# Attention and channel-mixing block: the first products directly behind score 3, the weight differences in other banks, and the first two projections later

## The reference

```python
def layernorm(x): return (x - mean(x)) / sqrt(var(x) + 1e-5)

def attention(x, weight):                 # b=4, t=1024, c=128, nh=16, hs=8
    y = x.reshape(b, t, nh, hs).transpose(0, 2, 1, 3)
    attn = softmax(einsum('bhtk,bhsk->bhts', y, y) / sqrt(hs))
    o = einsum('bhts,bsc->bhtc', attn, x)            # all 128 channels for each head
    return o.transpose(0, 2, 1, 3).reshape(b, t, nh * c) @ weight

def channel_mix(x, W_r, W_k, W_v, mu_r, mu_k):
    x_prev = x shifted by one token, zeros ahead of it
    xr, xk = mu_r*x + (1-mu_r)*x_prev, mu_k*x + (1-mu_k)*x_prev
    return sigmoid(xr @ W_r.T) * (relu(xk @ W_k.T)**2 @ W_v.T)

x = x + layernorm(attention(layernorm(x), weight))
x = x + layernorm(channel_mix(layernorm(x), ...))
```

## Time and profile before

| | |
|---|---|
| time, median of 3 | 944.18 us (943.57 to 948.45) |
| profiled execution | 950.29 us, of it a span of 948.5 us |
| TensorE busy | 914.9 us (96%) |
| VectorE busy | 850.3 us (90%) |
| ScalarE busy | 753.4 us (79%) |
| GpSimd busy | 320.2 us (34%) |

### The profile page before, as it was taken

The page is one execution under the profiler, slowest core; times in us unless marked ns, Lnnn a source line. Parts: engine busy times, 40 slices in busy tenths (PEclk is TensorE's granted clock), DMA queues, the critical chain, the costliest instruction groups (busy, mean ns, idle before and its releaser), DMA issues.

```text
span 948.5 us, 17874 instructions
## 1 busy us (share of the span) xinstructions
PE 914.9 (96%) x6065; PEld 441.9 (47%) x6065; DVE 850.3 (90%) x1117; ACT 753.4 (79%) x1048; POOL 320.2 (34%) x485
## 2 busy tenths in 40 slices
PE   3999999999999999999999999999999999999995
PEld 2444444444544444444444444544544444444453
DVE  7889898899898899989988979989889899898887
ACT  6787878788778778888778887889787978788855
POOL 2111432441143613515115282443313451153501
PEclk9999999999999999999999999999999999999999
DMA  5899999989889888999988978899988989889840
GB/s 162 195 225 188 205 197 200 226 190 204 177 173 201 163 181 174 208 193 207 185 178 179 203 157 179 176 222 202 206 173 180 188 182 188 172 179 201 174 81 24
DMA packets 98698, 173.12 MB, mean 183 GB/s; under 512 B 21040, under 2 KB 61360, under 8 KB 98608
## 3 DMA queue, kind: packets, MB, share of 16 engines
q0 software_dynamic: 36720, 133.71, 72.3%
q1 hardware_dynamic: 61888, 38.28, 14.7%
HBM read 27.72 MB, written 10.49 MB: 40 GB/s over the span
## 4 chain that ended last, share of the span: by engine, by line
PE 80%; issue 5%; POOL 4%; DVE 4%; DMA 4%; ACT 4%; DVEq 0%; POOLq 0%; ACTq 0%
PE ps_o L610 22%; PE ps_o L612 20%; PE ps_o L611 20%; PE ps_s L591 7%; DMA e_hi<-e_f 3%; PE ps_r L625 3%; PE ps_r L627 3%; PE ps_r L626 3%; ACT e_f L776 2%; DVE e_lo L1129 1%; POOL zT L452 1%; POOL e_hi L433 1%; PE ps_x L652 1%; PE ps_x L648 1%; POOL fnw L411 1%
## 5 line engine op out<-in xcount | busy, mean ns | idle before, releaser
L1129 DVE TENSOR_TENSOR e_lo<-e_f,e_hi 128x2048 f16<-128x2048 f32 x256 | 586.1, 2290 | 62.2 <-DMA e_hi<-e_f 62.1
L776 ACT ACTIVATE e_f<-ps_s 128x2048 f32<-128x2048 f32 x256 | 481.6, 1881 | 133.8 <-PE ps_s L591 124.4
L610 PE MATMUL ps_o<-e_hi,y_hi 128*128 128x512 f16 x1024 | 390.7, 382 | 6.3 <-DVE o_neg L1135 4.7
L612 PE MATMUL ps_o<-e_hi,y_lo 128*128 128x512 f16 x1024 | 388.1, 379 | 0.0
L611 PE MATMUL ps_o<-e_lo,y_hi 128*128 128x512 f16 x1024 | 388.1, 379 | 0.0
L433 POOL DMA_DIRECT2D e_hi<-e_f x255 | 140.9, 553 | 571.1 <-ACT e_f L776 469.8
L610 PEld LDWEIGHTS ps_o<-e_hi,y_hi 128*128 128x128 f16 x1024 | 99.7, 97 | 155.0 <-issue 56.1
L788 ACT ACTIVATE part<-ps_r,rden 128x128 f32<-128x128 f32 x508 | 144.8, 373 | 33.3 <-DVE rden L1141 32.6
L612 PEld LDWEIGHTS ps_o<-e_hi,y_lo 128*128 128x128 f16 x1024 | 100.2, 98 | 120.9
L611 PEld LDWEIGHTS ps_o<-e_lo,y_hi 128*128 128x128 f16 x1024 | 100.4, 98 | 91.5 <-issue 0.7
L591 PE MATMUL ps_s<-op_t,op_s 32*128 32x512 f16 x1024 | 102.5, 388 | 2.9 <-ACT e_f L776 2.4
(11 more groups left out here) (235 smaller groups left out, 507.4 us busy)
## 6 DMA issues: line engine op xcount, KB each, us to landing
e_hi<-e_f POOLq DMA_DIRECT2D x255, 512.0 KB, 5.1
op_t<-scr_t SPq DMA_DIRECT2D x496, 32.0 KB, 3.7
op_s<-scr_s SPq DMA_DIRECT2D x496, 16.0 KB, 3.3
scr_s<-yT SPq DMA_DIRECT2D x12, 256.0 KB, 2.9
scr_t<-yT SPq DMA_DIRECT2D x12, 256.0 KB, 5.4
out_dram<-res SPq DMA_DIRECT2D x7, 256.0 KB, 4.6
xs<-in_L_attn_x_dram SPq DMA_DIRECT2D x3, 512.0 KB, 6.2
scr_s<-eighth SPq DMA_DIRECT2D x4, 256.0 KB, 4.4
```

The costliest lines, as they stand in the source:

```text
L610: nc.tensor.matmul(dst, y_hi[:, b % 2, s, :], e_hi[:, ring, g, :], start=(q == 0 and g == 0), stop=False)
L612: mm = nc.tensor.matmul(dst, y_lo[:, b % 2, s, :], e_hi[:, ring, g, :], start=False, stop=(q == 1 and g == 3))
L776: nc.scalar.activation(e_f[:, k % EF_RING], ps_s[:], ACT.Exp, scale=1.0 / ROOT).then_inc(weighed, 1)
L1129: dve.tensor_tensor(flat(e_lo[:, ring]), flat(e_f[:, k % EF_RING]), flat(e_hi[:, ring]), ALU.subtract).then_inc(split, 1)
```

## The change

The change rearranges the opening. On TensorE `products(0)` moves from counter 4, where it stood behind two of the weight differences, to counter 3, directly behind `score(3)`. The weight differences go to other banks and places: before, differences 0 and 1 both used `ps_o[1]`, so that 1 waited for `weight_base(0)`; now they use `ps_o[1]`, `ps_r`, `ps_x`, `ps_r`, and the last one stands behind `products(2)`. The weight sum moves from `ps_r` to `ps_x` and one counter later. On VectorE the four `weight_base` stand one behind each of the splits of quads 1 to 4; before, two of them stood ahead of the split of quad 1. `weight_scale`, `weights_high`, `weights_neg` and `weights_low` all stand two counters later. The first two projections with their `invert`, `scale` and `add` stand one counter later (10 and 11 for `project`, where they were at 9 and 10); from step 2 on nothing moves.

```diff
--- before.py
+++ after.py
@@ -242,13 +242,13 @@
             return (b, k % (2 * PER_ROW)) if b < B else (None, None)
 
         def weights_ps(i):
-            return (ps_o[:, 1, :], ps_o[:, 1, :], ps_r[:], ps_x[:])[i]
+            return (ps_o[:, 1, :], ps_r[:], ps_x[:], ps_r[:])[i]
 
         def step_at(k, lead):
 
-            if k == lead + 1:
-                return 0
-            return (k - lead) // 2 if k > lead and (k - lead) % 2 == 0 else None
+            if k in (lead + 2, lead + 3):
+                return k - lead - 2
+            return (k - lead) // 2 if k > lead + 3 and (k - lead) % 2 == 0 else None
 
         def batch_of(j):
             return j // (2 * H)
@@ -526,7 +526,7 @@
             def weight_sum():
                 pe.wait_ge(w_squared, 1)
                 pe.wait_ge(w_based, 3)
-                nc.tensor.matmul(ps_r[:, 0:1], ones[:], w_sum[:, 0:1], start=True, stop=True).then_inc(w_total, 1)
+                nc.tensor.matmul(ps_x[:, 0:1], ones[:], w_sum[:, 0:1], start=True, stop=True).then_inc(w_total, 1)
 
             def first_operands(n):
                 pe.wait_ge(comb_s_ok, n + 1)
@@ -562,11 +562,11 @@
                     pe.wait_ge(w_in, 16)
                     pe.wait_ge(shift_ready, 1)
                 if i == 1:
-                    pe.wait_ge(w_based, 1)
+                    pe.wait_ge(first_s_in, 2)
                 if i == 2:
-                    pe.wait_ge(first_s_in, 2)
+                    pe.wait_ge(first_t_in, 3)
                 if i == 3:
-                    pe.wait_ge(first_t_in, 3)
+                    pe.wait_ge(w_based, 2)
                 nc.tensor.matmul(weights_ps(i), less[:], flat(w_raw[:, 4 * i:4 * i + 4, :]), start=True,
                                  stop=True).then_inc(w_less, 1)
 
@@ -601,7 +601,7 @@
                     if j == 0:
                         pe.wait_ge(yT_ready, 1)
                     if j == 1:
-                        pe.wait_ge(w_based, 2)
+                        pe.wait_ge(w_based, 1)
                     if j % (2 * H) == 0:
                         pe.wait_ge(y_marked, b + 1)
                 dst = ps_o[:, j % 2, :]
@@ -666,15 +666,17 @@
                 if k == 2:
                     turn_shift(0)
                 if k == LAG - 1:
+                    products(0)
+                    first_operands(1)
                     weights_less(0)
-                    first_operands(1)
+                if k == LAG:
                     weights_less(1)
-                if k == LAG:
                     weights_less(2)
-                    weights_less(3)
-                if 0 <= k - LAG < QUADS:
+                if 1 <= k - LAG < QUADS:
                     products(k - LAG)
                 if k == LAG + 2:
+                    weights_less(3)
+                if k == LAG + 3:
                     weight_sum()
                 if k == 12:
                     turn_ffn_weights()
@@ -849,7 +851,7 @@
 
             def keep_weight_sum():
                 act.wait_ge(w_total, 1)
-                nc.scalar.activation(w_sum[:, 1:2], ps_r[:, 0:1], ACT.Copy).then_inc(w_summed, 1)
+                nc.scalar.activation(w_sum[:, 1:2], ps_x[:, 0:1], ACT.Copy).then_inc(w_summed, 1)
 
             def normalize_half():
                 act.wait_ge(centred, 1)
@@ -898,11 +900,11 @@
                     take_second_t()
                 if k == 4:
                     square_weights()
-                if k == 6:
+                if k == 8:
                     keep_weight_sum()
-                if k == 7:
+                if k == 9:
                     weights_high()
-                if k == 8:
+                if k == 10:
                     weights_neg()
                 if k == 12:
                     turn_in_ffn_weights()
@@ -1246,13 +1248,11 @@
                     split_quad(k - 2)
                 if k == 2:
                     first_operands(1)
-                    weight_base(0)
-                    weight_base(1)
-                if k in (3, 4):
-                    weight_base(k - 1)
-                if k == 6:
+                if 3 <= k < 7:
+                    weight_base(k - 3)
+                if k == 8:
                     weight_scale()
-                if k == 8:
+                if k == 10:
                     weights_low()
                 for r, o in rows_at(k):
                     row_part(o, r)
```

## The result

The changed kernel takes 955.25 us (median of 4, 955.08 to 957.45), the kernel before 944.84 beside it (median of 4, 943.57 to 948.45): a ratio of 1.010, 95% interval 1.0072 to 1.0127. A second comparison of the same pair, the run after_again, gave 1.0092 (1.0065 to 1.0118), 8.7 us. It is slower, the way the forecast said, and inside the range, though only 0.25 us under its upper end. Of the cases named it is not the one called likeliest: the clock did fall in the wait.

The account below looks back on a forecast made before the run. TensorE's queue was taken as the bound: `score(13)` at 68.5 against 60.91 is 7.6 us late, less 0.3 for an earlier rate rise, 7.3; on the median 944.2 that makes 951.5 us, range 947 to 955.5.

Parts of the forecast that it names:

- The bound: TensorE, busy 96%, sets the end; time it loses before `score(13)` stays lost unless a later wait takes it back.
- The new wait: Before `project(0)`, TensorE waits for `weights_low` from 52.0 to 56.7: 4.7 us.
- the next one in the row: Before `project(0)`, if `weights_low` were through by 53.5, only `weights_neg` would be waited for: 1.3 us.
- The lower bound of 3.3 us: Shortest wait expected before `project(0)`, since VectorE was taken not to be free before about 50.5.
- The order of scaling 1: Before `project(2)`, `scale(1)` stands behind ScalarE's take of the FFN weights and `take_o(3)`; TensorE waits 2.3 us.
- The 0.8 us before `project(1)`: TensorE's wait for `scale(0)` until 61.3; the like wait before the change was 0.89 us.
- From score(3) to score(8): In the opening, products at half rate and ScalarE's squares make `score(4)` 1.9 us late and `score(8)` 1.1 us late.
- "Worth 0" for the order of the weight bases: VectorE's 2.53 us standing before the second `weight_base` goes, but nothing on the path waits for it: worth 0.
- The fall of the clock: Rival, chance 0.24: TensorE's rate halves in the wait before `project(0)`, costing 3 us; 10.3 in all, 954.5.
- The likeliest case: The forecast itself, chance 0.50: waits of 4.7 and 2.3 us before projections, 7.3 us slower in all, 951.5.
- The short wait: Rival, chance 0.14: `weights_low` through by 53.5, so `project(0)` waits only for `weights_neg`; 947 to 948.4.
- The giving back: Rival, chance 0.08: steady-part waits shrink and return the lateness, deciding at 2.6 us; with all 6.1, 945.4.

Follow-up runs that it names:

- filled: Changed kernel plus 22 idle matmuls into the free bank `ps_x` before `project(0)`; ratio to the kernel before 1.0047.
- low_early: Changed kernel with `weights_low` one counter earlier (9 instead of 10), ahead of the split of quad 8; ratio to the kernel before 1.0032.
- weights_later: Kernel before with the later weights' steps and the first two projections one counter later, without the opening's order and banks; ratio 1.0067.
- filled_both: Changed kernel plus idle matmuls into `ps_x` in both waits, 22 before `project(0)` and 7 before `project(2)`; ratio to the kernel before 1.0044.
- proj_later: Kernel before with only the first two projections, their inverses, scalings and additions one counter later; ratio 1.0033.
- scale_first: low_early with ScalarE's scaling 1 ahead of the take of the FFN weights and take 3 at counter 12; ratio to the kernel before 1.0014.
- opening: Kernel before with the opening's new order on TensorE alone; banks, VectorE's order and projections as before; ratio 1.0031.
- mix_scale: Kernel before with changed opening, banks and base order, last difference at counter 5, scaling 0 ahead of take 2 at counter 10; ratios 0.9989 and 0.9997.
- xs_first: Changed kernel with the load of the second batch's `x` at counter 0 of SyncE's loop instead of 6; ratio to the kernel before 1.0102.

## Why the prediction was right, and where it was not

**The bound** held for the change: what TensorE loses up to `score(13)` is lost in the end. 8.4 and 8.2 us in the profiles are 8.7 (6.2 to 11.2) in the second comparison; the first one's medians are 10.4 apart, with an interval of 6.8 to 12.0, so the 2 us above the profile are within chance. That 955.25 still lies inside the range, whose upper end is 955.5, is therefore partly luck. For filled the rule didn't hold: 8.9 us late at `score(14)`, 4.5 (2.7 to 6.3) in the time.

**The new wait** was right in place, kind and about in size: 5.40 against 4.7. `project(0)` started at 56.53, where I had 56.7: the conversion was issued 1.0 us sooner than in my sum (44.61) and took 0.5 longer to land, and 0.25 passed between the end of `weights_low` and the projection, which I had left out. So the closeness of 56.53 to 56.7 is partly errors that cancel. The wait is longer because `products(6)` ended 0.9 us sooner, at 51.1 instead of 52.0. low_early confirms the next one in the row, 1.80 us for `weights_neg`, against 1.3. The lower bound of 3.3 us is near the shortest wait seen (3.32 in weights_later) but rests on a wrong reading: I had VectorE busy until about 50.5 as before, where `weights_low` stood ahead of the split of quad 7. With `weights_low` gone behind it was free at 49.8, and in filled_both and weights_later it began the split of quad 8 at 49.46 and 48.65.

**The order of scaling 1** was right: 2.3 forecast, 2.25 measured, alone in proj_later, gone in scale_first. The 0.8 us before `project(1)` didn't come: at half rate the products ahead of it took longer.

**From score(3) to score(8)** I had 1.1 us of lateness, measured 0.2. The rate rose before the products ended and the transposes took 1.0 us instead of the 1.5 that I read from ScalarE's start. The clock is where the doubt had been put, and I had taken 0.3 of a possible 1.2. The comparison has its own chance in it: of the three profiles with the old order of that stretch, the kernel before's has the latest `score(4)`, by 0.7 and 1.2 us.

**"Worth 0" for the order of the weight bases** was wrong, as the run opening shows: without it, and the banks that go with it, TensorE would have been 3.1 us later at `score(10)`. Nor was VectorE's standing gone: it waits 2.9 us for the weight differences in the changed kernel. The term hid because I priced it against the kernel before, where nothing waited, instead of against the opening's new order, which makes VectorE wait.

**The fall of the clock** I gave 0.24 and 3 us. It came in both profiles of the changed kernel, and costs 1.1 (filled_both against the changed kernel). The mechanism was right, the price too high by two things: the rate rose 4.0 us after `project(0)` began and not after 5.9, so that the work took 1.7 us longer and not 3, and 0.6 of that lies under a wait for `scale(0)`, as the argument against it had said. It fell 2.6 us after the last product, where the end of the trace before had 4.6 us without work. The likeliest case's 7.3 and this 1.1 make the 8.4. The case that happened was the rival, with a price between the two.

**The short wait** did not happen. **The giving back** isn't seen in the times of the changed kernel, but the sign that I had named for being wrong, a shift that shrinks towards the end, did appear: from 8.4 to 4.8 us, and from 8.2 to 4.4 in after_again. As a sign it was a poor one. It is measured against one execution of the kernel before with much waiting in its steady part (8.0 us, not the 6.1 of the two waits that I counted), and the two profiles of mix_scale differ by 6.3 us with the same instructions. Whether some of it is given back all the same, as the run filled suggests, is open.

## What to carry to other kernels

When a step is moved by so many places and what waits for it by fewer, the slack is the difference: here the weights' steps went two counters and their reader one, and the reader had had none to spare. Price a reordering against the order in which it will stand: the bases' new place, with its banks, was worth up to three microseconds beside the new place of the products. And look one step behind a wait that you add: what an in-order engine has queued behind it (here `scale(1)` behind two other evictions) is the next wait.

## What was not expected

TensorE's clock can fall to the half level on a wait as short as 2.25 us: it did in low_early and xs_first, where the wait's first matmul already goes at half rate (rows of 0.27 and 0.26 us instead of 0.22), and in proj_later and filled, 0.5 to 0.6 us behind that matmul. It did not on the same wait in the changed kernel, after_again and weights_later, nor on the 1.80 us in low_early and scale_first. The Trainium skill (TensorE: Matmul & The Clock Gate, "HAM oscillation") tells the mechanism, a wait between groups of matmuls making the rate fall and the warm-up due again. The runs agree on that, though the waits in its example are longer than 2.25 us, and they show that what a fall costs depends on what else the engine would wait for, 1.1 to 1.6 us here. With both waits filled with idle matmuls the clock did not fall (filled_both, one profile), which is worth 1.1 of the 2.4 to 2.6 us by which `score(13)` came sooner. Why the same wait makes the clock fall in one run and not in another is open.

The granted clock's column shows full speed in the opening as well, where matmuls go at half rate until 24 to 28 us, depending on the run; there the durations decide.
